# Convolution on one core: one product of 512 columns into an unused bank at the head of nine units

## The reference

```python
x = lax.conv_general_dilated(inputs, conv_w, window_strides=(1,), padding='SAME',
                             dimension_numbers=('NWC', 'WIO', 'NWC')) + conv_b
q, k, v = jnp.split(x, 3, axis=-1)
...
x = _layernorm(x + _L0_attn_ref(x, ...), axis=-1)
x = _layernorm(x + _L0_ffn_ref(x, ...), axis=-1)
```

## Time and profile before

| | before |
|---|---|
| median of 3 runs | 1571.21 us (1571.04 to 1571.63) |
| profiled execution, its own time | 1571.44 us |
| its span | 1569.6 us |
| TensorE busy | 1542.9 us (98%), 10816 products |
| VectorE busy | 1182.0 us (75%) |
| ScalarE busy | 610.7 us (39%) |
| mean granted TensorE clock | 0.995 |

### The profile page before, as it was taken

One profiled execution on the slowest core, in us unless ns is written; L12 is line 12 of the kernel. 1 busy time (PEld: TensorE's weight loads), 2 busy tenths in 40 slices (PEclk: granted clock), 3 DMA queues, 4 the chain that ended last, 5 costly groups with the idle time before them and its releaser, 6 DMA issues. The chain is left out here.

```text
span 1569.6 us, 29296 instructions
## 1 busy us (share of the span) xinstructions
PE 1542.9 (98%) x10816; PEld 1383.5 (88%) x10816; DVE 1182.0 (75%) x2795; ACT 610.7 (39%) x1740; POOL 256.8 (16%) x232
## 2 busy tenths in 40 slices
PE   7999999999999999999999999999999999999997
PEld 7999999999978888888888887799998999989997
DVE  8879868878886666666666677688878888788885
ACT  4224223421566767676776777211111111111110
POOL 0000000000000001010000113433333333333331
PEclk9999999999999999999999999999999999999999
DMA  8988765688810101101010222311221112211111
GB/s 324 371 294 303 270 212 184 208 309 282 280 69 1 55 1 53 53 0 53 0 53 0 68 101 70 115 61 61 73 77 60 60 60 73 77 60 60 60 52 46
DMA packets 55301, 181.05 MB, mean 115 GB/s; under 512 B 5568, under 2 KB 13888, under 8 KB 48704
## 3 DMA queue, kind: packets, MB, share of 16 engines
q1 hardware_dynamic: 53504, 173.81, 31.3%
q10 hardware_dynamic: 1728, 6.29, 1.0%
HBM read 125.49 MB, written 54.53 MB: 115 GB/s over the span
## 5 line engine op out<-in xcount | busy, mean ns | idle before, releaser
L990 ACT ACTIVATE scores_and_probs<-scores_and_probs,score_neg_max 128x128 f32<-128x128 f32 x512 | 197.9, 391 | 2.4 <-DVE score_neg_max L1089 2.4
L959 POOL TENSOR_TENSOR weights<-conv_tile,weights 128x1024 fp32r<-128x1024 f32 x14 | 35.6, 2545 | 860.0 <-ACT weights L976 775.8
L1445 ACT ACTIVATE gate_exp<-h_and_gate,gate_neg_max 128x8 f32<-128x8 f32 x32 | 9.6, 300 | 347.8 <-DVE gate_neg_max L1523 347.8
L1084 DVE CUSTOM_DVE_ANT_0 scores_and_probs<-bankb,causal_mask 128x128 f32<-128x128 f32 x256 | 59.2, 287 | 111.7 <-PE bankc L1211 111.3
L383 ACT ACTIVATE x_split<-x_planes 128x1024 fp32r<-128x1024 f32 x47 | 49.9, 1062 | 179.4 <-PE bankf L660 153.4
L1178 PE MATMUL bankg<-weights 128*128 128x512 f32 x378 | 103.2, 408 | 0.3 <-DVE v_heads L1074 0.2
L1197 PE MATMUL bankh<-weights 128*128 128x512 f32 x384 | 98.1, 391 | 1.7 <-DVE probs_T L1102 1.7
L1197 PE MATMUL banka<-weights 128*128 128x512 f32 x384 | 98.3, 392 | 1.0 <-POOL weights L959 0.8
L990 ACT ACTIVATION_READ_ACCUMULATOR scores_and_probs<-scores_and_probs,score_neg_max 128x1 f32 x512 | 97.7, 191 | 0.0
L514 DVE TENSOR_TENSOR x_split<-x_planes,x_split 128x1024 fp32r<-128x1024 f32 x47 | 57.4, 1222 | 45.7 <-ACT x_split L383 45.6
L1609 PE MATMUL bankc<-weights 128*128 128x512 f32 x384 | 90.5, 391 | 0.0
(11 more groups left out here) (242 smaller groups left out, 3857.4 us busy)
## 6 DMA issues: line engine op xcount, KB each, us to landing
x_raw<-in_xT SPq DMA_DIRECT2D x31, 1028.0 KB, 7.4
conv_tile<-in_x SPq DMA_DIRECT2D x32, 512.0 KB, 3.6
out<-out_tile SPq DMA_DIRECT2D x32, 512.0 KB, 2.7
conv_tile<-convT_scratch SPq DMA_DIRECT2D x16, 768.0 KB, 6.7
ce_scratch<-conv_l SPq DMA_DIRECT2D x16, 512.0 KB, 7.4
x_planes<-ce_scratch SPq DMA_DIRECT2D x16, 512.0 KB, 5.2
conv_y<-in_conv_w SPq DMA_DIRECT2D x6, 1152.0 KB, 7.8
convT_scratch<-conv_y SPq DMA_DIRECT2D x12, 512.0 KB, 6.9
```

The source lines that it names most:

```text
L959: nc.gpsimd.tensor_tensor(cs[:, LO, a:b, :], craw[:, a:b, :], cs[:, HI, a:b, :].bitcast(F32), ALU.subtract).then_inc(c_lo, 1)
L990: last = nc.scalar.activation(probs[:, s % 2, i, :], probs[:, s % 2, i, :], ACT.Exp, bias=ntop[:, s % 2, i:i + 1], scale=SCORE_SCALE, accu ...
L1084: last = nc.vector.tensor_tensor_reduce(out=probs[:, s % 2, i, :], in0=ps_s[h][:, n * P:(n + 1) * P], in1=mask[:], scale=1.0, scalar=LOWES ...
```

## The change

At the first granule of units 1, 2, 3, 5, 6, 7, 9, 10 and 11 (granules 4, 8, 12, 20, 24, 28, 36, 40 and 44), after the wait for x, TensorE waits for banks a and b as the next product does and makes one product of 512 columns: it loads 128 weight columns of the first chunk and streams 512 columns of the same weights into bank g. Nobody reads the result; the attention stage overwrites it.

```diff
@@
     WR = 3
     KTAPS = CF * P
+    WIDE = [GRAN * u for u in range(U) if u % NU]
@@
             if u > 0 and f % 2 == 0:
                 pe.wait_ge(evac, FP * (u - 1) + f // 2 + 1)
 
+        def widen(u):
+            wait_bank(u, 0)
+            nc.tensor.matmul(attn.banks[CF][:], w[:, 0, HI, 0, 0:P], w[:, 0, HI, 0, 0:ST], start=True, stop=True)
+
         for u in range(U):
             for g in range(GRAN):
                 j = GRAN * u + g
                 chunks = range(CPG * g, CPG * g + CPG)
                 if j > 0:
                     pe.wait_ge(x_lo, j + 1)
+                if j in WIDE:
+                    widen(u)
```

## The result

| | before | after |
|---|---|---|
| median of 20 runs each | 1565.65 us (1556.1 to 1572.09) | 1572.59 us (1570.94 to 1574.46) |
| ratio after / before | | 1.0042, 95% interval 1.0024 to 1.0061 |
| profiled execution, its own time | 1571.44 us | 1573.9 us |
| its span | 1569.6 us | 1572.1 us |

The change makes the kernel slower by 0.4%. The forecast was 1560.7 us and faster.

A forecast was written before the change was run, and what follows sets the result against it. TensorE's stream was taken to bound the kernel: −12.8 us from the tight pace, +2.04 for nine wide products and +0.3 for what is late next gave −10.5, 1571.21 to 1560.7 us. Range 1558.8 to 1573.5 us.

The forecast's parts named there:

- What bounds the kernel: TensorE, busy 98% of the span; its convolution stream is tight (8.16 us a granule) or loose (8.48) after a stall.
- Own time of the wide product: On TensorE at nine unit heads: 0.227 us each, 2.04 us in all, all of it on the path.
- Its waits: At the nine unit heads: it takes over waits the first product already has, costing nothing beyond its own time.
- What it may set off: In the convolution: a wide product returns the loose stream to the tight pace, 40 granules x 0.32 = −12.8 us.
- Unit 1 as the exception: At granule 4, directly behind the stall: the wide product probably doesn't settle the pace; the one at granule 8 should.
- What is late next: After the faster convolution: no new stall at granule 19, but 0.3 us lost waiting for VectorE at attention's start.
- A: Rival for the whole change: it only costs, 1573.3 us, or 1572.3 in an instruction-issue variant; together 33%.
- C: Rival at each wide product: it acts as a restart, 9 x 0.42 = 3.8 us slower, 1575.0 us; 7%.

The follow-up runs named there:

- early_copy: Kernel before, no wide product, ScalarE copying banks a and b out before its x_split of granule 5, removing the granule 4 stall: median 1559.35 us, ratio 0.9962.
- only_second: Kernel of the change with only the 512-column product at granule 8 kept: 1569.22 to 1570.82 us, ratio 1.0031 against before.
- before_again: The kernel before, unchanged, run and profiled once more: 1556.82 to 1570.95 us, 4 of 12 runs tight.
- ladder_restore: early_copy plus 512-column products at 15 granules, each followed one granule later by one of 272 to 496 columns; one profiled execution, no time given.
- ladder_again: early_copy plus products of 512, 480, 448, 400, 384 columns, three times each, each followed one granule later by one of 320; no time given.
- ladder_knock: early_copy plus products of 272 to 512 columns at 15 granules, each followed one granule later by one of 320; one execution, no time given.
- early_copy_nine: early_copy with all nine 512-column products added: 1571.29 to 1574.07 us, median 1572.37, 0 of 12 runs tight.
- only_first: Kernel of the change with only the 512-column product at granule 4 kept, behind the stall: median 1561.98 us, ratio 0.9984 against before.
- nine_256: Kernel of the change with its nine added products at 256 columns instead of 512: 8 of 12 runs 1557.85 to 1562.58 us, others 1571.49 to 1572.71.

## Why the prediction was wrong

**What bounds the kernel**: right. TensorE's stream has two paces, 8.16 and 8.48 us a granule, and they are worth 14 us up to the start of attention (417.20 against 403.08 in early_copy). The medians of before's two groups lie 10.3 us apart (1570.3 and 1560.0). But I read one profile and three runs near 1571 as what the kernel is. It is tight in 59 of 130 runs. A stall doesn't always drop the stream into the loose pace, it draws anew: only_second's execution was tight behind its stall at granule 4, and before_again's went from loose to tight behind its wait at granule 1. With a tight half the kernel had something to lose, and no rival of mine took it.

**Own time of the wide product**: right in size. 0.227 us behind a loose stream, 0.232 behind a tight one.

**Its waits**: right; it added none.

**What it may set off**: this step failed, with its sign. I put: "in the steady loose state one product suffices to clear whatever is late". In 21 places of the profiles a 512-column product came upon a loose stream in full run, and it never restored it. In 18 places it came upon a tight one and each time left it loose: 12 in ladder_restore, 3 in ladder_again, one each in ladder_knock, early_copy_nine and only_second. The evidence that I used could not bear it. The six 512-column products behind the loose stretch show how wide products run behind narrow loose ones, not how the narrow ones run behind a wide one, and the slow start showed a tight stream behind long products only once. The start of the kernel after refutes that too: the distances between products fall from 213 ns over 180 to 115, 120, 117 and stay at 118, where those of before fell over 131, 119, 115 to 113. TensorE's timeline of the kernel after, (14.14 − 13.44) / 6 = 0.117:

```profile
13.44 0.87 PE L661 MATMUL banke<-x_split,weights 128*128 128x256 f32 x6
14.14 0.87 PE L661 MATMUL bankf<-x_split,weights 128*128 128x256 f32 x6
```

**Unit 1 as the exception**: of no weight, but for another reason than the one given: behind the stall 7 of 12 runs with a wide product are tight.

**What is late next**: no new stall, right. In early_copy 47 granules in a row took 8.16 us. The 0.3 us at the start of attention can't be read: from there to the end the profiled executions take between 1149.8 and 1158.2 us.

**The rivals.** A came near the time (1573.3 against 1572.59) with its mechanism only in part: the wide product costs its own time in loose runs, and makes the others 12.6 us later (1572.59 against 1560.0, the median of before's faster ten). As half of the runs of before are tight, the medians differ by 7 us and the ratio by 0.4%. C, the slower rival, had a wrong mechanism: no wide product cost 0.35 us itself, the dearest 0.31 behind the stall in only_first. The range held the time, but from a base that was one of two. The missing case was "the wide product throws a tight stream out": 2 us slower in a run that would be loose anyway, and up to 14.1 + 2.0 = 16 us slower in one that would be tight.

The weight load as long as the product, which the prediction took from the Trainium skill (page "TensorE: Matmul & The Clock Gate", section "LDWEIGHTS (loading the stationary operand)"), fits the fact that 256-column products keep either pace for hundreds of products. No row gives a load's own time: the loads are recorded with 187 to 193 ns while they follow each other every 113 or 118. The rule did not tell which way a disturbance goes. The other rule that the prediction took from the Trainium skill (same page, section "Step-by-step: what each phase is for"), that the queue pulls weight loads ahead by itself, restored nothing in an unbroken stream of any profile: no loose stream came back between two added products.

**What stays open**: why 512, 480 and 400 columns make the stream loose and 448 and 320 don't. On a tight stream 480, 400 and 448 columns did the same in 4 places of 4 each and 512 in 18 of 18, so it isn't chance, but by what mechanism the width decides, no run shows. Open too is what decides the pace behind a stall: of the four at granule 4 without an added product one left the stream tight and three loose.

## What to carry to other kernels

In a long stream of equal products, each with its own weight load, read the distance between starts of products over the whole stream and in several executions: two profiles of the same kernel may differ by the pace alone, and a few equal runs don't prove that there is only one. A disturbance in such a stream (a stall, one odd product) can move it either way for hundreds of products, so test the neighbours of its size too. Here 320 columns in place of 512 in all nine places turned a loss of 0.4% into a gain of 0.3%, and one such product at granule 4 gained 0.4%.

## What the runs showed of the hardware

- A stream of 256-column products, each with a weight load of 128 columns, has stable paces of 113.3 and 117.8 ns at full clock. After the rise of the clock the pace changed, in the convolutions of the 16 profiles, only at a stall of TensorE or at a product of another width.
- Out of the slow clock (213 ns a product) the stream came tight in 14 profiled executions and loose in two (after and before_again). A wait at full clock can change it in both directions: tight to loose in before at granule 4 and in nine_256 at granule 1, loose to tight in before_again at granule 1.
- The effect of one odd product is exact: 512 columns made a tight stream loose in 18 of 18 places, 320 left it tight in all 38 places in the running stream, and brought a loose one back behind 512 (5 of 5) and 480 (4 of 4), never behind 400 (0 of 4).
